# A feature-interaction tower on one core: one of five row groups moves from a matmul to a DMA, the row splits and VectorE's sums move in the order

## The reference

```python
z0 = einsum('bid,bjd->bdij', x0, x0).reshape(B, D, 39 * 39)
cur0 = relu(einsum('bdk,kl->bld', z0, W0))            # W0: 1521 x 128
next_h, direct0 = split(cur0, 2, axis=1)              # 64 + 64 rows
z1 = einsum('bid,bjd->bdij', x0, next_h).reshape(B, D, 39 * 64)
cur1 = relu(einsum('bdk,kl->bld', z1, W1))            # W1: 2496 x 128
z = sum(concat([direct0, cur1], axis=1), axis=-1)     # 192 features
h = relu(concat([z, dense_ctx]) @ W_top1 + b_top1)    # 512
h = relu(h @ W_top2 + b_top2)                         # 256
y = h @ W_top3
```

## Time and profile before

| engine | busy us | share | what |
|---|---|---|---|
| TensorE | 406.2 | 93% | matmuls |
| VectorE | 347.9 | 80% | 80 multiplications, 64 low parts of 2.28 us each |
| ScalarE | 225.6 | 52% | squares, high parts |
| GpSimd | 284.5 | 65% | 176 gathers, until 341 us |
| DMA queue of SyncE | 60.76 MB | 51% of 16 engines | 48 wide groups of 1 MB |

### The profile page before, as it was taken

The page is one execution under the profiler, slowest core; times in us unless marked ns, Lnnn a source line. Parts: engine busy times, 40 slices in busy tenths (PEclk is TensorE's granted clock), DMA queues, the critical chain, the costliest instruction groups (busy, mean ns, idle before and its releaser), DMA issues.

```text
span 437.2 us, 4204 instructions
## 1 busy us (share of the span) xinstructions
PE 406.2 (93%) x1490; PEld 250.0 (57%) x1490; DVE 347.9 (80%) x196; ACT 225.6 (52%) x224; POOL 284.5 (65%) x180
## 2 busy tenths in 40 slices
PE   0587699799999999999999999999999999998897
PEld 0454356456566656565656565665656565665464
DVE  0304664799999998989898989898989898999900
ACT  2115445365655647483747464738374656553422
POOL 5778887888888888888888888888888100000000
PEclk9989899899999999999999999999999999999999
DMA  8383549594848383838384747475675638350000
GB/s 284 107 195 61 127 107 224 137 219 135 209 122 220 92 235 77 237 82 222 107 222 122 220 116 208 120 201 142 164 179 155 183 116 220 105 184 0 1 0 2
DMA packets 25524, 64.04 MB, mean 146 GB/s; under 512 B 7779, under 2 KB 15928, under 8 KB 19743
## 3 DMA queue, kind: packets, MB, share of 16 engines
q1 hardware_dynamic: 19156, 60.76, 51.4%
q0 software_dynamic: 5632, 1.35, 2.9%
q10 hardware_dynamic: 715, 1.66, 1.1%
HBM read 59.88 MB, written 3.85 MB: 146 GB/s over the span
## 4 chain that ended last, share of the span: by engine, by line
PE 78%; POOL 12%; issue 4%; DMA 3%; DVE 2%; ACT 0%; DVEq 0%; ACTq 0%
PE acc L497 16%; POOL found L276 12%; PE acc L529 12%; PE acc L521 12%; PE acc L522 12%; PE acc L540 10%; PE sums L480 6%; PE acc L536 4%; PE spread L510 3%; DMA found<-in_table_dram,rows_sb 2%; PE spread L569 2%; DVE z_lo L419 2%; DVE z L411 1%; DMA base_sb<-in_base_dram 1%; PE sums L558 1%
## 5 line engine op out<-in xcount | busy, mean ns | idle before, releaser
L276 POOL DMA_INDIRECT found<-in_table_dram,rows_sb x176 | 284.3, 1615 | 56.7 <-issue 53.4
L319 ACT ACTIVATE z_hi<-z 128x2048 fp32r<-128x2048 f32 x64 | 122.4, 1913 | 82.6 <-DVE z L411 82.6
L419 DVE TENSOR_TENSOR z_lo<-z,z_hi 128x2048 fp32r<-128x2048 f32 x64 | 146.2, 2285 | 14.6 <-ACT z_hi L319 14.6
L521 PE MATMUL acc<-z_hi,w_hi 128*128 128x512 f32 x256 | 106.8, 417 | 5.4 <-ACT cur L312 3.1
L497 PE MATMUL acc<-squares,w 128*128 128x512 f32 (+1 forms) x224 | 110.8, 612 | 0.0
L411 DVE TENSOR_TENSOR z<-x_wide,h 128x2048 f32<-128x2048 f32 x48 | 109.6, 2282 | 0.0
L522 PE MATMUL acc<-z_hi,w_lo 128*128 128x512 f32 x256 | 100.9, 394 | 0.0
L411 DVE TENSOR_TENSOR z<-spread,h 128x2048 f32<-128x2048 f32 x32 | 73.1, 2286 | 20.9 <-ACT h L303 16.8
L295 ACT ACTIVATE squares<-sums 128x1024 f32<-128x1024 f32 x64 | 58.4, 913 | 58.9 <-PE sums L480 58.9
L529 PE MATMUL acc<-z_lo,w_hi 128*128 128x512 f32 x256 | 82.2, 443 | 0.6 <-DVE z_lo L419 0.6
L529 PEld LDWEIGHTS acc<-z_lo,w_hi 128*128 128x128 f32 x256 | 48.0, 189 | 24.1 <-issue 15.1
(11 more groups left out here) (44 smaller groups left out, 146.3 us busy)
## 6 DMA issues: line engine op xcount, KB each, us to landing
x_wide<-x_rows SPq DMA_DIRECT2D x48, 512.0 KB, 4.5
x_wide<-x_rows SPq DMA_DIRECT2D x80, 256.0 KB, 5.2
x_parts<-x_rows SPq DMA_DIRECT2D x32, 128.0 KB, 2.6
x_wide<-x_rows SPq DMA_DIRECT2D x16, 192.0 KB
found<-in_table_dram,rows_sb POOLq DMA_INDIRECT x176
x_rows<-found SPq DMA_DIRECT2D x32, 80.4 KB
w_sb<-in_w_dram SPq DMA_DIRECT2D x1, 1280.0 KB, 6.6
x_rows<-found SPq DMA_DIRECT2D x16, 73.1 KB
```

Source lines behind the costliest of these rows:

```text
L276: pool.indirect_dma_start(out=found[:, b, 2, s * D:s * D + D], out_offset=None, in_=table, in_offset=bass.IndirectOffsetOnAxis(ap=rows_sb[ ...
L319: nc.scalar.activation(z_hi[:, n % RING], z[:, n % RING], ACT.Copy).then_inc(hi_done, 1)
L419: nc.vector.tensor_tensor(z_lo[:, n % RING], z[:, n % RING], z_hi[:, n % RING], ALU.subtract).then_inc(lo_done, 1)
L521: nc.tensor.matmul(acc1[:, :], w1_hi[:, t, :], z_hi[:, r, a, :], start=(t == 0), stop=False)
```

## The change

`SPREAD` has one group (0) and `WIDE` four (1, 2, 3, 4); which features lie in which group changes with the tables, the amount of arithmetic does not. So group 3's `spread_out` goes, and a fourth 1 MB `widen` comes for every chunk. The gathers stay as they are. The first chunk's order on TensorE and ScalarE is written out anew, `split(1)` and `split(2)` move (to before `multiply(0)` and before `multiply(4)` on VectorE), and from then on `split(c+2)` stands in step g = 0 of chunk c, in place of `split(c+3)` at the end of chunk c; `bring(c+2)` is ahead of the loads of chunk c + 1. VectorE's `reduce0(c+1)` and `reduce1(c-1)` stand one behind the other in step g = 4, ahead of `low_part`.

```diff
--- before.py
+++ after.py
@@ -43,10 +43,10 @@
 
 G = 5
 T1 = G * QUADS
-SPREAD = [0, 3]
-WIDE = [1, 2, 4]
-SPREAD_FROM = [0, 4, 32, 12]
-WIDE_FROM = [[8, 16], [28, 35], [20, 24]]
+SPREAD = [0]
+WIDE = [1, 2, 3, 4]
+SPREAD_FROM = [0, 14, 16, 37]
+WIDE_FROM = [[2, 6], [30, 33], [10, 18], [22, 26]]
 
 
 WHOLE = 2
@@ -255,12 +255,17 @@
             widen(0, 1)
             bring(1)
             widen(0, 2)
+            widen(0, 3)
+            widen(1, 0)
+            widen(1, 1)
             bring(2)
-            for c in range(CHUNKS - 1):
+            widen(1, 2)
+            widen(1, 3)
+            for c in range(1, CHUNKS - 1):
+                if c + 2 < CHUNKS:
+                    bring(c + 2)
                 for i in range(len(WIDE)):
                     widen(c + 1, i)
-                if c + BUFS < CHUNKS:
-                    bring(c + BUFS)
             sp.wait_ge(y_ready, 1)
             sp.dma_start(out, y_sb[:, :]).then_inc(out_done, 16)
             sp.wait_ge(out_done, 16)
@@ -349,29 +354,32 @@
             split(0)
             for d in range(ND):
                 square(d)
+            split(1)
             evict0(0)
-            split(1)
             high_part(0)
-            high_part(1)
-            square(ND)
-            square(ND + 1)
             for c in range(CHUNKS):
                 for g in range(G):
                     n = G * c + g
                     if g == 0 and c:
                         evict1(c - 1)
+                    if g == 0 and c < 2:
+                        square(ND * (c + 1))
+                    if n == 0:
+                        high_part(1)
+                    if g == 0 and c < 2:
+                        square(ND * (c + 1) + 1)
                     if g < 2 and c + 1 < CHUNKS:
                         square(ND * (c + 1) + 2 + g)
-                    if g > 2 and c + 2 < CHUNKS:
+                    if g > 2 and 0 < c < CHUNKS - 2:
                         square(ND * (c + 2) + g - 3)
                     if 0 < n < G * CHUNKS - 1 and is_v(n + 1):
                         high_part(n + 1)
-                    if g == 2 and c + 1 < CHUNKS:
+                    if g == (2 if c else 3) and c + 1 < CHUNKS:
                         evict0(c + 1)
-                    if n == 1:
+                    if n == 2:
                         split(2)
-                    if g == G - 1 and c + BUFS < CHUNKS:
-                        split(c + BUFS)
+                    if g == 0 and 0 < c < CHUNKS - 2:
+                        split(c + 2)
                     if c == CHUNKS - 1 and g > 2:
                         for m in [[0, 1], [2, 3]][g - 3]:
                             hid1_act(m, early)
@@ -446,25 +454,28 @@
                                     ALU.subtract).then_inc(w1_lo_ready, 1)
 
             dve.wait_ge(select_ready, 1)
+            split(1)
             multiply(0)
-            split(1)
             for c in range(CHUNKS):
                 for g in range(G):
                     n = G * c + g
+                    if n == 3:
+                        split(2)
                     if n + 1 < G * CHUNKS:
                         multiply(n + 1)
+                    if g == G - 1 and c + 1 < CHUNKS:
+
+                        reduce0(c + 1)
+                        if c:
+                            reduce1(c - 1)
                     if is_v(n):
                         low_part(n)
                     if n == 0:
                         reduce0(0)
-                    if n == 1:
-                        split(2)
-                    if g == 1 and c:
-                        reduce1(c - 1)
-                    if g == G - 1 and c + 1 < CHUNKS:
-                        reduce0(c + 1)
-                    if g == G - 1 and c + BUFS < CHUNKS:
-                        split(c + BUFS)
+                    if g == 0 and 0 < c < CHUNKS - 2:
+                        split(c + 2)
+                    if n == G * (CHUNKS - 1) + 1:
+                        reduce1(CHUNKS - 2)
             reduce1(CHUNKS - 1)
 
         @block.tensor
@@ -595,16 +606,32 @@
             keep_busy(acc1, 14)
             pe.wait_ge(w1_in, 16)
             pe.wait_ge(w1_lo_ready, 1)
-            for c in range(CHUNKS):
+            add_up(ND)
+            contract1_hi(0)
+            add_up(ND + 1)
+            contract0(ND)
+            contract1_lo(0)
+            contract1_hi(1)
+            add_up(ND + 2)
+            contract0(ND + 1)
+            contract1_lo(1)
+            add_up(ND + 3)
+            contract0(ND + 2)
+            contract1_whole(2, ND + 3)
+            spread_out(G)
+            contract1_hi(3)
+            contract1_lo(3)
+            contract1_hi(4)
+            for c in range(1, CHUNKS):
                 for g in range(G):
                     n = G * c + g
-                    if n == 0:
-                        contract1_hi(0)
-                        add_up(ND)
-                        add_up(ND + 1)
-                        contract0(ND)
-                    elif g == 0:
+                    if n == G:
+                        add_up(2 * ND)
+                    if g == 0:
                         contract1_lo(n - 1)
+                    if n == G:
+                        add_up(2 * ND + 1)
+                        contract0(2 * ND)
                     if (n + 2) % G in SPREAD and n + 2 < G * CHUNKS:
                         spread_out(n + 2)
                     if g < 2 and c + 1 < CHUNKS:
```

## The result

The median is 465.79 us (459.28 to 467.1, four runs) beside 440.48 for the kernel before on the same chip: ratio 1.0551, interval [1.0504, 1.0598]. 430 was predicted. The profiled execution is the slowest of the four, 467.1 us with a span of 465.0; that of before has 437.2.

A forecast was written before the change was run, and what follows sets the result against it. The prediction took TensorE's own work to bound the 13 steady periods, with gathers setting the startup. Steady -6.8, start -3.2 and tail +0.6 sum to -9.4, so 439.2 becomes 430 us; range 425 to 440.

The forecast's parts named there:

- 8 + 3 = 11 again: GpSimd, each period: eight VectorE blockers (both inputs in SBUF) pass one gather each, other stretches three; no loss.
- The forecast's own signs of being wrong: Steady chunks and GpSimd: a period above 22.9 us, or gathers that end after 350 us.
- the 0.95: GpSimd beside VectorE's SBUF work: a delayed gather ends about 0.95 us after one of VectorE's instructions has ended.
- The sums thus cost nothing: VectorE, each period: both sums, 1.3 us, fill the 1.15 us the low part had waited for z_hi.
- the count of eleven: GpSimd: a chunk's eleven gathers still fit into one period, forecast at 22.36 us.
- Steady TensorE, -6.8: TensorE, 13 periods: removing group 3's `spread_out` saves 0.52 us each, 22.88 to 22.36.
- Start, -3.2: Startup up to the mark of chunk 1: earlier splits bring that mark to 89.7 us, saving 3.2 us.
- Tail, +0.6: After the last mark: VectorE's last sum has one more sum ahead of it, 0.6 us; tail at 47.4.
- The DMA ring: Rival: gathers sharing DMA engines with wide loads land only when the burst ends, delaying the split; 449 us, chance 0.13.
- VectorE as the bound: Rival: 0.6 us of cover fails, TensorE waits for each low part, period near 22.8; 436 us, chance 0.2.

The follow-up runs named there:

- e10: Changed kernel with VectorE waiting for its own two sums ahead of the low part (and in chunk 0): 439.05 us, 0.9984 of the kernel before.
- e14: e10 with ten gathers a chunk in place of eleven from chunk 3 on: 437.24 us, 0.9931 of the kernel before.
- e15: e10 with group 3's wide loads bringing one of their four tiles from chunk 1 on: 439.15 us, 0.9997 of the kernel before.
- e18: e10 with both the ten gathers of e14 and the short loads of e15: 434.05 us, 0.9869 of the kernel before.
- e13: Changed kernel with VectorE waiting for its own multiplication ahead of group 0's low part, inside the run: 456.08 us, 1.0341 of the kernel before.
- e17: e10 with VectorE's part of the split moved one multiplication later, behind that of group 2: 435.72 us, 0.9911 of the kernel before.
- e1: Changed kernel with both sums ahead of the multiplication from spread instead of behind it: 460.0 us, 1.0468 of the kernel before.
- e3: Changed kernel with one small VectorE product (128x2 elements) per chunk between the last sum and the low part: 462.57 us, 1.0528 of the kernel before.
- e4: Changed kernel's order with groups 0 and 3 spread by TensorE, so three wide groups: 460.99 us, 1.0504 of the kernel before.
- e9: Changed kernel with splits where the kernel before has them and the low part ahead of both sums: 463.6 us, 1.0431 of the kernel before.
- e5: Kernel before with only VectorE's two sums moved together ahead of the last group's low part: 449.8 us, 1.0191 of the kernel before.
- e12: Kernel before with only the groups changed (one spread, four wide), its order kept: 449.91 us, 1.0258 of the kernel before.

## Why the prediction was wrong

- **The step that failed** is the one on GpSimd: "8 + 3 = 11 again: no loss, but with little to spare. If a slot is lost, the missing one is bought by VectorE's idling, at most 0.3 us a period." It took for granted that a blocker lets one gather through at its end. In the new order a gather starts just behind the start of a run of three blockers that is entered without a gap, and most of these got through at none of the ends inside it; each such gather costs two slots, 4.2 us of GpSimd, with none to spare. (Two slots: 7.07 where e10's gather in the same place took 2.85.) GpSimd's busy time rose by 35.7 us; eleven such gathers make 46 of extra time, and the other 165 averaged 1.47 us, where the kernel before has 1.60. The 13 periods took 318.0 us where 290.7 were forecast; 20.2 of these 27.3 us are what e10 wins back. The forecast's own signs of being wrong came: a mean period of 24.46, and gathers until 377.2 us.
- The kernel before had one such gather, in a stretch that the forecast did not read. GpSimd, then VectorE:

```profile
47.26 4.69 POOL L276 DMA_INDIRECT found<-in_table_dram,rows_sb  x1 [0.30 <-issue]
```
```profile
46.00 0.67 DVE L424 TENSOR_REDUCE feat_b<-direct 64x32 f32<-64x512 f32 x1
46.60 2.27 DVE L411 TENSOR_TENSOR z<-x_wide,h 128x2048 f32<-128x2048 f32 x1
48.80 2.27 DVE L419 TENSOR_TENSOR z_lo<-z,z_hi 128x2048 fp32r<-128x2048 f32 x1
```

It passed the end at 48.80 and ended at 51.95, 0.95 behind the run. One row was also read a little wrong: at 125.3 a multiplication ended and a low part began; the 0.95 stands.
- "The sums thus cost nothing" was true of VectorE: the low part starts in time and TensorE does not wait for it in an undisturbed period. But the hole that they filled was the gap by which the gathers got in, as e10 shows: it gives back 0.17 us of it. The 1.15 us in the earlier trace rows looked like idle time and had a use on another engine.
- Even without that the count of eleven was too good, by 0.4 us a chunk (22.68 against 22.26 in e10), and stores land late; together 8.4 us over the 13 periods, of which leaving out a gather alone gave back 2.1 (e14) and shorter loads alone 0.8 (e15).
- **Steady TensorE, -6.8**: right. 22.26 was measured, 22.36 forecast; over 13 periods 8.1 us are to be had (e18: 289.4 against 297.5).
- **Start, -3.2**: wrong, +1.7. The gathers of chunk 2 ended at 56.8 in place of 54.5 (one of 6.89 us at 47.31), ScalarE's split of it waited 2.76 and VectorE's came at 62.9, 60 forecast. And I had no term for the clock:

```profile
75.00:85.00 10.00, 8.40 (x22) 4.63 (x22) 3.29 (x3) 5.60 (x6) 8.48 (x6) 0.74 0.20 37
```

TensorE stood between small pieces of work and was granted 0.74 here. Two kernels with the same order at the start and almost the same time of VectorE's split of chunk 2 show what that is worth: e13 (62.38, clock 1.00) has the mark of chunk 1 at 91.96, e18 (62.44, clock 0.66) at 94.86. So the lower clock goes with 2.9 us, and the rest of the miss is put down to the later split, which is not shown by itself. The kernel before has 0.83 in this stretch, so part of its own start is of this kind. At the best (e10, 91.32) the start gains 1.6.
- **Tail, +0.6**: VectorE's part right (TensorE's wait for the sum 2.20), but 52.35 in place of 47.4:

```profile
428.63 1.94 PE L569 MATMUL sums<-feat_b,wt1b_sb 80*128 80x480 f32 x2 [2.20 <-DVE feat_a L438]
...
435.80 4.26 PE L551 MATMUL acc<-z,w_sb 128*128 128x512 f32 x6
```

The two f32 matmul pairs of L569 took 1.94 in place of 1.04; from 425.74 to 438.82 the granted clock was 0.61. In e10, e14, e15, e17 and e18 the tail is 47.6 to 49.3, but in e1, e3, e4 and e9, with periods as long as the change's, it is 48.7 to 49.1. So the long periods alone do not make 52.35, and why the clock fell that far in this execution stays open.
- **The rivals.** The DMA ring (449 us) was not the cause: the loss stays with three wide groups (e4) and goes with four (e10). A part of its mechanism is seen once the gathers keep pace: from 104 us on the stores of e14 landed after 3.2 to 9.1 us, where the changed kernel's took 2.7 to 3.3. VectorE as the bound did not come. That gathers are delayed at all beside instructions with both inputs in SBUF holds in every trace here; all of these gathers also read `rows_sb` in SBUF, and what happens to one that reads nothing there no run shows.

## To carry to other kernels

Before filling an idle microsecond of VectorE, ask who uses it: where GpSimd issues indirect DMAs beside VectorE's SBUF work, do not count one slot for each of VectorE's instructions where a run of them is entered without a wait. A wait of VectorE for its own last result is a gap of 0.1 to 0.2 us that can be placed where it is wanted. When two resources are each within 2% of the bound, relieving one (e14, e15) shows almost nothing; relieve both before judging either.

## What the runs showed of the hardware

- 78 gathers in the twenty traces were kept out of a run of VectorE's instructions with both inputs in SBUF: they took 4.69 to 5.00 us (two large instructions), 7.07 (three large instructions), 9.79 (four), 11.73 (five and a split), 16.55 (a split and seven), 18.34 (eight and a split). All started between 0.05 us ahead of the run and 0.67 behind its start, and in no case had VectorE waited at the entry. Of 214 gathers that started in the same stretch of a run entered with a wait none was kept out.
- That is not yet the whole condition: 54 gathers that met a run entered without a wait in the same stretch were let in at its first end. Of these 35 stood where a multiplication from `x_wide` follows the one from `spread` (2 others there were kept out, in e5), 12 are those of e12. What tells them apart stays open.
- A wait of VectorE for as little as 0.05 us at the entry was enough (the changed kernel at 151.45), and one of 0.11 us inside the run (e13); a small instruction was not (e3).
- The clock of the start can't be foretold from the time of the split: from 75 to 85 us it was 1.00 in e1, whose VectorE split of chunk 2 came at 63.72, and 0.69 in e4, whose came at 61.89.
- The wide loads took 4.5 and 5.2 us to land before (512 and 256 KB) and 6.9 and 9.3 after, though the bytes rose by 1 MB a chunk only: that with four groups the next chunk's loads are issued while the last ones run is my reading, not tested. With a quarter of the fourth group's bytes (e15) they took 8.1 and 9.1.
